# Three product buffers for two, four C rows for five, and an earlier place for the gate's transposes with a later one for a projection

## The reference, cut to what matters

```
x  = einsum('ed,bld->bel', in_proj_w, ctx)          # the front: projection,
u  = silu(conv4(x) + conv_b)                        # four taps, silu
dt, Bm, Cm = split(einsum('ke,bel->bkl', x_proj_w, u))   # 32, 16, 16 rows
delta = softplus(einsum('er,brl->bel', dt_proj_w, dt) + dt_proj_b)
state = state * exp(delta * A) + (delta * u) * B    # for 16 states n, over l
y  = sum_n state_n * C_n + D * u
y  = y * silu(layernorm(x_in))                      # the gate
x1 = x_in + swap(y)
out = x1 + layernorm(x1) @ W.T + b + sum of the two best experts' (A, B) products
```

## Time and profile before

| | before |
|---|---|
| median of three runs | 2175.45 us (2169.37 to 2175.68) |
| the profiled execution | 2179.93 us, with a span of 2178.1 us |
| PE, DVE, POOL, ACT busy | 1812.5, 1789.7, 1774.2, 1255.9 us |
| mean granted TensorE clock | 0.906 of full speed |

### The profile page before, as it was taken

The page is one execution under the profiler, slowest core; times in us unless marked ns, Lnnn a source line. Parts: engine busy times, 40 slices in busy tenths (PEclk is TensorE's granted clock), DMA queues, the critical chain, the costliest instruction groups (busy, mean ns, idle before and its releaser), DMA issues.

```text
span 2178.1 us, 23728 instructions
## 1 busy us (share of the span) xinstructions
PE 1812.5 (83%) x7992; PEld 1097.9 (50%) x7992; DVE 1789.7 (82%) x1430; ACT 1255.9 (58%) x1701; POOL 1774.2 (81%) x798
## 2 busy tenths in 40 slices
PE   9877777777778888888888888888888888878999
PEld 3344444454455555555555555555555545555554
DVE  3589898888898899987999999987999999997111
ACT  3355555456566666655766666655766666663432
POOL 0389888889898998988999998988999999997300
PEclk9777787778779999998999999998999999999999
DMA  4665555576755656685666665685755556665300
GB/s 157 242 233 189 188 180 185 180 247 245 236 189 183 208 205 210 224 282 212 221 207 210 214 206 205 222 277 176 240 195 202 201 205 213 213 213 193 136 29 34
DMA packets 157977, 435.88 MB, mean 200 GB/s; under 512 B 14528, under 2 KB 47552, under 8 KB 157728
## 3 DMA queue, kind: packets, MB, share of 16 engines
q1 hardware_dynamic: 157856, 434.37, 58.1%
HBM read 383.46 MB, written 50.86 MB: 199 GB/s over the span
## 4 chain that ended last, share of the span: by engine, by line
DVE 33%; PE 30%; POOL 15%; issue 13%; ACT 6%; DMA 4%; SPq 0%; DVEq 0%; POOLq 0%; ACTq 0%
DVE state L1051 21%; POOL prod L1188 10%; DVE row L1036 9%; PE bank_a L548 7%; PE y_ps L492 6%; POOL drive_rows L1181 3%; PE bank_b L443 3%; DVE conv L1028 3%; PE bank_b L548 3%; PE row L570 3%; DMA xrow<-in_x 2%; ACT decay L807 2%; PE bank_b L472 2%; PE row L486 1%; PE bank_b L452 1%
## 5 line engine op out<-in xcount | busy, mean ns | idle before, releaser
L1188 POOL TENSOR_TENSOR prod<-state,c_rows 128x1024 f32<-128x1024 f32 x512 | 1201.2, 2359 | 163.4 <-PE y_ps L492 132.9
L1051 DVE TENSOR_TENSOR_SCAN state<-decay,row 128x1024 f32<-128x1024 f32 x332 | 758.0, 2283 | 9.5 <-POOL prod L1188 2.4
L492 PEld LDWEIGHTS y_ps<-ident,prod 128*128 128x128 f32 x4096 | 516.7, 152 | 343.3 <-issue 173.9
L492 PE MATMUL y_ps<-ident,prod 128*128 128x128 f32 x4096 | 596.9, 294 | 82.8 <-POOL prod L1188 81.2
L1036 DVE TENSOR_TENSOR row<-du,row 128x1024 f32<-128x1024 f32 x332 | 402.1, 1211 | 105.5 <-PE row L486 102.9
L1051 DVE TENSOR_TENSOR_SCAN state<-row,drive_rows 128x1024 f32<-128x1024 f32 x180 | 409.8, 2277 | 21.8 <-POOL drive_rows L1181 21.5
L1181 POOL TENSOR_TENSOR drive_rows<-du,b_rows 128x1024 f32<-128x1024 f32 x180 | 425.4, 2364 | 2.0 <-DMA b_rows<-bc_d 2.0
L807 ACT ACTIVATE row<-delta,a 128x1024 f32<-128x1024 f32 x180 | 201.0, 1117 | 389.2 <-DVE state L1051 388.8
L548 PE MATMUL bank_a<-w_o,xnT 128*128 128x512 f32 x816 | 400.2, 622 | 30.1 <-DVE x L1098 30.1
L807 ACT ACTIVATE decay<-delta,a 128x1024 f32<-128x1024 f32 x332 | 372.2, 1135 | 0.1
L486 PE MATMUL row<-parts,sel 96*128 96x512 bf16 x664 | 221.7, 418 | 119.4 <-DVE state L1051 114.4
(11 more groups left out here) (131 smaller groups left out, 1653.1 us busy)
## 6 DMA issues: line engine op xcount, KB each, us to landing
c_rows<-bc_d SPq DMA_DIRECT2D x512, 512.0 KB, 4.3
xrow<-in_x SPq DMA_DIRECT2D x32, 512.0 KB, 6.6
skip<-u_d SPq DMA_DIRECT2D x32, 512.0 KB, 5.8
yy_d<-yy SPq DMA_DIRECT2D x32, 512.0 KB, 6.2
b_rows<-bc_d SPq DMA_DIRECT2D x24, 512.0 KB, 6.0
u_d<-conv SPq DMA_DIRECT2D x24, 512.0 KB, 5.3
ctx<-u_d SPq DMA_DIRECT2D x48, 256.0 KB, 5.9
x<-in_x SPq DMA_DIRECT2D x24, 512.0 KB, 5.9
```

The costliest lines, as they stand in the source:

```text
L492: last = nc.tensor.matmul(y_ps[:, i * P:(i + 1) * P], source[:, i * P:(i + 1) * P], ident[:, :], start=(first and i % (H // P) == 0), stop ...
L1051: nc.vector.tensor_tensor_scan(state[:, q % STATES, :], factor, term, 0.0, ALU.mult, ALU.add).then_inc(scan_done, 1)
L1188: nc.gpsimd.tensor_tensor(prod[:, q % PRODS, :], state[:, q % STATES, :], c_rows[:, q % RING, :], ALU.mult).then_inc(prod_ready, 1)
```

## The change

`RING` goes from 5 to 4 and `PRODS` from 2 to 3, so the two tiles together keep their size. `turn_gate` of the second half moves from TensorE's section 4 to 3, and its `take_gate` from ACT's section 5 to 4. In the `SPREAD_OUT` blocks the first front half's pieces k = 0 to 3 stand in sections 2, 3, 4 and 4, not in 0, 1, 2 and 3; its first tap (ACT) and its other taps (DVE) move from section 5 to 6. The expression in `project`'s call is rewritten so that two pieces can share a section; for `IN_ONE_GO` it gives what it gave.

```
-RING, DECAYS, STATES, PRODS, DRIVES = 5, 4, 3, 2, 2
+RING, DECAYS, STATES, PRODS, DRIVES = 4, 4, 3, 3, 2
...
-SPREAD_OUT = (((0, 1, 2, 3), (5, 6, 7, 8), (9, 10, 11, 12)), (5, 10, 14), (5, 10, 15))
+SPREAD_OUT = (((2, 3, 4, 4), (5, 6, 7, 8), (9, 10, 11, 12)), (6, 10, 14), (6, 10, 15))
...
-                if m in (2, 4):
-                    turn_gate(E, m // 2 - 1)
+                if m in (2, 3):
+                    turn_gate(E, m - 2)
...
-                        project(E, i, [at.index(m)] if len(at) > 1 else range(NK))
+                        project(E, i, [k for k in range(NK) if at[k % len(at)] == m])
...
-                if m in (3, 5):
-                    take_gate(E, (m - 3) // 2)
+                if m in (3, 4):
+                    take_gate(E, m - 3)
```

## The result

The changed kernel takes 2115.3 us (median of 4 runs, 2111.18 to 2118.18) against 2175.56 us (4 runs, 2169.37 to 2183.69): ratio 0.9727, 95% interval 0.9699 to 0.9755. The forecast was 2120 us. The profiled execution took 2111.18 us (span 2109.3, clock 0.913).

The account below looks back on a forecast made before the run. Bound: a ring of DVE, POOL and TensorE, waits counting only where DVE or POOL stands still. Terms 12.0 + 7.8 + 3 + 24.6 + 2.5 + 8 + 2 - 4 = 55.9 us gave 2120 us, range 2092 to 2155 us.

Parts of the forecast that it names:

- The gate: Mostly dense blocks: an earlier second gate copy removes TensorE's and DVE's waits, 1.58 us in most; 24.6 us in all.
- the clock term: Blocks 9, 12 and 20: TensorE's lower clock just after the gate wait; half of 5.1 us gained, 2.5 us.
- This sign of being wrong: DVE waits in section 15 that grow by what section 7 lost would show the forecast wrong.
- The first front half: Turns of blocks 1 to 5 and 8: pieces taken off the TensorE chain, 12.0 + 7.8 us.
- short turn: Blocks 1, 3 and 8: DVE's waits about 3.0 us, under the 4.0 us removed; 2.6 us gained each.
- all of it counts: Turns of blocks 2, 4 and 5: 4.0 us off the chain, less than DVE's wait; 12.0 us in all.
- only what the first term leaves can be gained: Blocks 2, 4 and 5: the third product buffer gains half of about 2 us left at each turn, 3 us.
- the third buffer: One more product buffer: early blocks 3 us, around 14/15 and 22/23 8 us, blocks 24 to 31 2 us.
- The wait for y: Sign of being right: DVE's wait in section 2 of blocks 2, 4 and 5 at about 1 us or less.
- rival A: Early blocks: TensorE's freed time returns as slow time, clock below 0.7, those gains vanish; 2145 us, chance 0.22.
- One C row fewer: At the start the fourth C row load stands behind w_o, cost 4 us; steady state 0.
- Rival C: Third buffer removes most of POOL's 132.9 us of waits, two thirds reaching the end, 88 us; 2087 us, chance 0.12.

Follow-up runs that it names:

- kernel 3: Original kernel with only the first front half's pieces moved to sections 2, 3, 4, 4: 2162.11 us, ratio 0.9938.
- kernel 5: Changed kernel with the second gate half's turn and copy back in their old sections: 2148.2 us, ratio 0.9885 to the original.
- kernel 6: Changed kernel with two product buffers and five C rows again: 2135.27 us, ratio 0.9827 to the original.
- kernel 9: Changed kernel with the first front half back in its old sections: 2122.71 us, ratio 0.9764 to the original.
- kernel 1: Original kernel with only three product buffers and four C rows: 2150.1 us, ratio 0.9884.
- kernel 4: Original kernel with only four C rows, two product buffers kept: 2180.2 us, ratio 1.0026.
- kernel 2: Original kernel with only the second gate half turned and copied one section earlier: 2150.88 us, ratio 0.9890.
- kernel 7: Changed kernel with the 4 MB of w_o and w_ra loaded in pieces in blocks 1 to 4: 2105.34 us, ratio 0.9689 to the original.
- kernel 10: Changed kernel with three C rows, the tile keeping four places: 2124.95 us, ratio 0.9769 to the original.

## Why the prediction was right, and where it was not

**The total.** Right, 2115.3 against 2120 us, but in part by luck: terms that were too large and terms that were too small made up for each other.

**The gate: right.** 24.6 us, with the clock term 27.1, against 24 to 34 us in four surroundings. The reading held link by link where I had read it: no wait of `bank_b`'s projection for the gate, no wait of DVE behind it, and 1.72 us off block 19's period where 1.6 was named. It is not the same 1.58 us eleven times. Blocks 17 and 21 moved only by 0.14 and 0.43 us, because the wait in section 15 grew by 1.39 and 1.27 us; blocks 13 and 20 lost most of their gain in the same way. This sign of being wrong came true in 5 of the 11 blocks (12, 13, 17, 20, 21). Blocks 9 and 10 gained more than forecast, 4.6 and 3.0 us, since their waits in section 15 shrank from 2.78 and 2.86 to 1.56 us each. No run separates the 2.5 us of the clock. In sum 9 to 13 gained 11.0 us against 9.6, and 16 to 21 7.0 against 10.3. That the edit is worth more with both others in place (1.58%) than alone (1.10%) is about as large as the uncertainty of such a difference.

**The first front half: too large, and the steps that failed.** The first is the 2.6 us for each short turn, 7.8 us in sum, a number between two ends and not a reading. Alone (kernel 3) the edit took 1.0 us off those three turns; the three long ones lost 9.7 us where "all of it counts" had 12.0. Alone the edit brought 13 us of the 19.8.

The second is the order of the two edits: "only what the first term leaves can be gained" by the third buffer, 3 us. No row supported that order. The buffers alone bring 16.3 us in blocks 1 to 5, all three edits 17.4: both shorten the same standstill. How much of it each would take depends on the gate's edit too (the small table behind kernels 5, 6 and 9). What the buffers do there is in part argued: POOL's products, and so the sums, are less late when the turn begins; but the clock at block 4's turn was also 1.00 in kernel 1 and 0.50 in before and after. The stage's sum, 20.2 us, was near, most likely because the stage's idle was the limit for both.

**The wait for y: wrong.** "About 1 us or less" in blocks 2, 4 and 5; it is 1.73, 1.72 and 1.73 us, and 2.63 us in blocks 3 and 8. In after the two waits of the long turns fell by 12.5 us in sum, so the 12.0 us are there; the short turns gave 2.0 us (3.15, 2.95 and 2.84 to 1.72, 2.63 and 2.63). What failed is the next step, that the third buffer would take half of the 2 us left in each of the long turns: beyond the 4.0 us it took 0 to 0.4. What is left is a `dt_half` of 2.00 us and a sum of 1.91 us at the lower clock level. In kernel 1 the same work took 1.05 and 0.89 us and DVE waited 0.38 us. This is the part of rival A that is true: the slow time stays at the turn. Its forecast was wrong. The early clock was not lower but 0.77 against 0.75, and the stage was not empty of gain.
In the Trainium skill ("TensorE: Matmul & The Clock Gate", What's actually happening) the lower clock is the default and activity lifts it. Rival A had concluded that spreading the work out would cost clock; the 0.77 doesn't show that, but the 2.00 us at the turn shows a place where the lower level remains.

**The third buffer: too small, in the early blocks and the last.** Forecast 9 us with the C row's cost, measured 12 to 27. Around 14/15 and 22/23 the forecast was 4 us each: kernel 1, with buffers only, gains 8.7 us (5.5 if the 3.2 above are taken off) and 4.9 us there. DVE waits 0.96 us in block 14 in place of 2.93, and POOL's longest wait for a sum is 1.70 us where before has three of more than 3. Block 15's 3.60 us is gone, and a wait of 1.65 us for ACT stands in its place; kernels 3 and 4 show nearly that with two product buffers (1.32 for the row, 1.55 and 1.53 for ACT), so it is not the third buffer's for certain. The early blocks are told of above.

**Blocks 24 to 31: 11.2 us against 2.** The four kernels with a third buffer (1, 5, 9 and after) gain 10.3, 8.1, 10.6 and 11.2 us there; the four with two buffers and another edit (4, 2, 6 and 3) 0.3, 3.0, 3.4 and 5.9. The groups don't overlap, so most of it is the buffer's, some 7 us on the average, more than the 2 us that I took from waits of 0.6 to 2.7 us a block. The rest moves from trace to trace.

**One C row fewer: right.** 5.6 us against 4; in after 11.85 of the 12.5 us of waiting are at the start, and no row is late in the dense blocks but one of 0.69 us. Kernel 7 confirmed that the big load ahead of it was the cause.

**The signs.** POOL's wait for TensorE was to fall below 40 us and fell to 9.1. Rival C had tied a gain of 88 us to that, two thirds of 132.9. The waits went and the 88 us did not come: 54 of the 123.8 us only changed their name. I had made the sign and the price one number. By the Trainium skill ("Perfetto Trace Analysis", Optimization Strategy) a repeated gap on the engine that should be saturated can mean too few buffers. That was true of the gap here: without the third buffer 83.0 to 134.7 us of this wait stay (kernels 2, 3, 4 and 6). What the trace adds is that less than 0.6 of it (69.8 of 123.8 us) became time, and this with two other edits. DVE's waits in section 15 kept their range, up to 2.9 us outside blocks 14 and 22, but moved between blocks, as told under the gate.

## What to carry to other kernels

Where two edits shorten the same standstill, bound the stage by its idle time and leave open which edit gets it: the sum for the early stage was good here, the sum per edit was not. In a ring of three engines, price a removed wait by what DVE or POOL stands still behind it in the same microseconds (1.58 us twice gave 1.72 us), and not by one line of the waits, which may only change its name: 123.8 us less there were 69.8 us less idle on POOL, 34.5 us more in kernel 10 were 13.9. Then look at the next wait in the same block: in five of eleven blocks it took back part or nearly all of the 1.58 us. The idle column of the group that runs through the whole main stage shows it. Look at what a small urgent load stands behind in its queue before paying for it with a buffer.

## What the runs showed of the hardware that was not expected

- One TensorE place, two prices: two `dt_half` matmuls took 2.00 us and a sum of eight 1.91 us in after, 1.05 and 0.89 us in kernel 1, at the same point of the program. The granted clock over these pieces was 0.50 and 1.00, the means over the stage 0.77 and 0.79: here the mean didn't tell which level the turn got.
- A 512 KB load behind 4 MB on one queue landed 22.8 us after issue, the same kind of load 4.3 us in the median over the run. Moving the big one away was worth 0.4% (8 to 10 us).
- Where an edit changes nothing in a stage, single traces still differ there: by 3.2 us at block 15, made up for by block 18, and by 0.3 to 5.9 us over blocks 24 to 31 (kernels 3 and 4). So a stage difference below some 6 us should not rest on one trace.
